# Deformable convolution main loop: distances and caps for two steps at a time, batches of eight, tap matmuls in two runs a block

## What is computed

```python
py = off_y + hs[None, None, :, None] + ky[None, :, None, None]
px = off_x + ws[None, None, None, :] + kx[None, :, None, None]
y0, x0 = jnp.floor(py), jnp.floor(px)
...
sampled = v00 * w00 + v01 * w01 + v10 * w10 + v11 * w11   # bilinear, zero outside the image
sampled = sampled * mask[:, None]
out = jnp.einsum('bckhw,ock->bohw', sampled, w.reshape(O, C, KK))
```

## Time and profile before

| what | value |
|---|---|
| median of three runs | 2331.67 us |
| lowest, highest run | 2330.77, 2337.22 us |
| span of the profiled execution, first to last instruction | 2334.2 us |
| PE, weight loads, DVE, ACT, POOL busy over the span | 66%, 45%, 67%, 62%, 26% |
| mean granted TensorE clock over the span | 0.846 |
| main loop, from the first `keep_even` to the last block | 701.8 to 2105.2 us |
| in it: PE, DVE, ACT, POOL busy | 1230.8, 1198.9, 1228.6, 570.8 us of 1403.4 |

### The profile page before, as it was taken

How to read it: one execution, slowest core, us unless ns; L and a number is a source line. 1 busy time by engine, 2 the same in 40 slices (tenths; PEclk the granted TensorE clock), 3 DMA queues, 4 the chain that set the end, 5 groups by cost and what they waited for, 6 DMA issues and landing times. The chain is left out here.

```text
span 2334.2 us, 61913 instructions
## 1 busy us (share of the span) xinstructions
PE 1539.5 (66%) x24206; PEld 1050.0 (45%) x24207; DVE 1558.4 (67%) x1718; ACT 1449.8 (62%) x2219; POOL 606.7 (26%) x1168
## 2 busy tenths in 40 slices
PE   4755980000008888888898898898888898891620
PEld 4632330000006666666665566666665666660310
DVE  5342006656717888888888788888887888883105
ACT  2221224344218898888898898898887898890102
POOL 2000000000033444444443444444444444430000
PEclk9688995555558999999999999999999999996555
DMA  2177874667675666666666666566666656640008
GB/s 116 32 190 184 233 218 159 215 227 275 235 214 126 151 147 157 149 149 155 150 148 152 148 149 157 149 150 157 149 146 150 152 147 157 149 100 22 3 0 338
DMA packets 288861, 362.19 MB, mean 155 GB/s; under 512 B 61853, under 2 KB 260820, under 8 KB 285014
## 3 DMA queue, kind: packets, MB, share of 16 engines
q1 hardware_dynamic: 209552, 226.57, 37.6%
q0 software_dynamic: 36864, 59.94, 11.2%
q10 hardware_dynamic: 42182, 72.05, 9.0%
HBM read 253.94 MB, written 104.39 MB: 154 GB/s over the span
## 5 line engine op out<-in xcount | busy, mean ns | idle before, releaser
L758 POOL DMA_DIRECT2D rows<-scratch_parts x1152 | 583.1, 514 | 821.1 <-PE ps_even_y L790 798.8
L799 PE MATMUL ps_odd_y<-rows,sel 32*128 32x504 f32 (+2 forms) x928 | 459.8, 496 | 502.5 <-DMA rows<-scratch_parts 345.2
L939 DVE TENSOR_TENSOR G<-odd_y,ps_odd_v 128x1008 f32<-128x1008 f32 (+2 forms) x464 | 542.0, 1168 | 182.5 <-PE ps_odd_v L816 182.4
L816 PE MATMUL ps_odd_v<-tent_x,stage 32*128 32x171 f32 (+2 forms) x5568 | 591.1, 318 | 0.0
L947 DVE TENSOR_TENSOR G<-even_v,ps_even_y 128x1008 f32<-128x1008 f32 (+2 forms) x464 | 539.3, 1162 | 23.6 <-ACT even_v L895 21.7
L816 PE MATMUL ps_even_v<-tent_x,stage 32*128 32x171 f32 (+3 forms) x5568 | 541.9, 324 | 8.5 <-DMA stage<-scratch_xt 8.3
L889 ACT COPY odd_y<-ps_odd_y 128x504 f32<-128x504 f32 (+2 forms) x928 | 526.4, 567 | 21.4 <-PE ps_odd_y L799 17.1
L895 ACT COPY even_v<-ps_even_v 128x1008 f32<-128x1008 f32 (+2 forms) x464 | 450.2, 970 | 134.6 <-PE ps_odd_v L816 126.5
L834 PE MATMUL ps_r<-G,conv_w 128*32 128x224 f32 (+1 forms) x8832 | 483.3, 346 | 13.2 <-ACT res L900 13.1
L799 PEld LDWEIGHTS ps_odd_y<-rows,sel 32*128 32x128 f32 x928 | 173.0, 186 | 689.8 <-issue 350.5
L816 PEld LDWEIGHTS ps_odd_v<-tent_x,stage 32*128 32x128 f32 x5568 | 477.8, 190 | 0.0
(11 more groups left out here) (134 smaller groups left out, 913.5 us busy)
## 6 DMA issues: line engine op xcount, KB each, us to landing
place<-scratch_px SPq DMA_DIRECT2D x960, 105.0 KB, 3.4
scratch_parts<-parts ACTq DMA_DIRECT2D x18, 3136.0 KB, 16.7
rows<-scratch_parts POOLq DMA_DIRECT2D x960, 52.5 KB, 3.4
x<-scratch_xh SPq DMA_DIRECT2D x48, 406.0 KB, 5.9
place<-scratch_px SPq DMA_DIRECT2D x192, 84.0 KB, 2.7
scratch_om<-om ACTq DMA_DIRECT2D x64, 196.0 KB, 7.1
rows<-scratch_parts POOLq DMA_DIRECT2D x192, 42.0 KB, 2.6
scratch_conv<-res SPq DMA_DIRECT2D x448, 14.0 KB, 1.8
```

What stands on the lines that cost most here:

```text
L758: pool.dma_start(bass.AP(tensor=rows[b][:].tensor, offset=32 * g * pitch + here, ap=[[2 * pitch, Y_KINDS], [GROUP * W, 3], [1, count * W]] ...
L799: nc.tensor.matmul(ps_odd_y[:, lo:hi], sel[32 * g:32 * g + 32, :], taps(rows, 32 * g, 32, p, lo, hi), start=True, stop=True).then_inc(odd_ ...
L816: m = nc.tensor.matmul(sub(ps_v[g // 2], 0, 128, i * 512 + lo + first, dims), stage[32 * g:32 * g + 32, j * IMAGE + v * C:j * IMAGE + (v + ...
L939: nc.vector.tensor_tensor(two(G, ROW, v, slot(v)), two(odd_y[p % 3], ROW, v), two(ps_v[1], 512, v), ALU.mult).then_inc(odd_weighted, 1)
```

## The change

Three things change in the main loop, and one beside it.

1. `distance` and `cap` handle two steps in one instruction. `dist_x` and `tent_x` hold 9 taps by two steps (1008 columns) in two buffers rather than 504 columns in three. A pair has 15 such twins, the last with a single step. They are issued in odd steps: step p computes the twin of steps p+3 and p+4; steps 27 and 28 compute the first two twins of the next pair.
2. Batches have 8 steps, not 5: four a pair (8, 8, 8, 5), with the same two buffers, so `place` and `rows` are loaded with 48 DMAs each a pair in place of 72, of 1.6 times the size.
3. A block's taps run in two runs, not four: in the second of its four steps taps 0 to 3, in the fourth taps 4 to 8. The first and third steps have none.
4. `zeros` shrinks, to make room; the far stage stores its pads in more, smaller DMAs.

```diff
-GROUP = 5
+GROUP = 8
...
-        zeros = sb("zeros", XT_ROWS * C)
+        zeros = sb("zeros", NEAR * C)
...
-            dist_x = [sb(f"dist_x{b}", ROW) for b in range(3)]
-            tent_x = [sb(f"tent_x{b}", ROW) for b in range(3)]
+            dist_x = [sb(f"dist_x{b}", 2 * ROW) for b in range(2)]
+            tent_x = [sb(f"tent_x{b}", 2 * ROW) for b in range(2)]
...
+            def twin(it, p):
+                return (STEPS + 1) // 2 * it + p // 2
+            def twin_steps(p):
+                return min(2, STEPS - p)
+            def sampled_by(n):
+                return STEPS * (n // TWINS) + min(2 * (n % TWINS + 1), STEPS)
+            def next_twin(it, p, last):
+                if p % 2 == 1 and p + 3 < STEPS:
+                    return it, p + 3
+                if p in (STEPS - 2, STEPS - 1) and not last:
+                    return it + 1, 2 * (p - STEPS + 2)
+                return None
...
-                                sp.wait_ge(distant, STEPS * it + p + 2)
+                                sp.wait_ge(distant, twin(it, p + 1) + 1)
...
-                    pe.wait_ge(tent_ready, n + 1)
+                    pe.wait_ge(tent_ready, twin(it, p) + 1)
...
-                        if at := block_of(it, p):
-                            if at[2] == 0:
+                        if (at := block_of(it, p)) and at[2] % 2:
+                            if at[2] == 1:
                                 pe.wait_ge(even_weighted, STEPS * at[0] + BLOCK // 2 * (at[1] + 1) + 1)
+                            reduce(at[0], at[1], at[2] - 1)
                             reduce(*at)
                         if to:
                             spread_odd(*to, 1)
...
                 def distance(it, p):
-                    n = STEPS * it + p
+                    n = twin(it, p)
...
                     wait(act, tent_ready, n - 1)
-                    lo, hi = both(p)
-                    nc.scalar.activation(sub(dist_x[p % 3], 0, 128, lo, [[W, (hi - lo) // W], [1, W]]),
-                                         taps(place, 0, 128, p, lo, hi), ACT.Abs, bias=at[:, 0:1]).then_inc(distant, 1)
+                    dims = [[2 * W, KK], [1, twin_steps(p) * W]]
+                    nc.scalar.activation(sub(dist_x[n % 2], 0, 128, 0, dims),
+                                         sub(place[p // GROUP % 2], 0, 128, p % GROUP * W, [[GROUP * W, KK], dims[1]]),
+                                         ACT.Abs, bias=at[:, 0:1]).then_inc(distant, 1)
...
-                        if to := ahead(it, p + 2, last):
+                        if (to := next_twin(it, p, last)):
                             distance(*to)
...
                 def cap(it, p):
-                    n = STEPS * it + p
+                    n = twin(it, p)
                     dve.wait_ge(distant, n + 1)
-                    wait(dve, sampled, n - 1)
...
+                    if n >= 2:
+                        dve.wait_ge(sampled, sampled_by(n - 2))
...
-                        if to := ahead(it, p + 2, last):
+                        if (to := next_twin(it, p, last)):
                             cap(*to)
```

More of the change, by code:

```diff
@@ L644, in program @@
             ASKED = {first + count - 2: n for n, (first, count) in enumerate(BATCHES)}
+            TWINS = (STEPS + 1) // 2
             block = st.enter_context(nc.Block())
@@ L651, in columns, with twin_part @@
                 return first * 3 * W, end * 3 * W
-            def both(p):
-                return columns(2 * p)[0], columns(2 * p + 1)[1]
+            def twin(it, p):
[4 more added lines that the diff above has]
+                return STEPS * (n // TWINS) + min(2 * (n % TWINS + 1), STEPS)
+            def twin_part(tile, part, parts, p, lo, hi, first, count):
+                return sub(tile, part, parts, lo * 2 + p % 2 * W + first, [[2 * W, (hi - lo) // W], [1, count]])
             def two(tile, pitch, v, offset=0):
@@ L814, in sample @@
                             lo, hi = columns(v)
-                            dims = [[W, (hi - lo) // W], [1, count]]
-                            m = nc.tensor.matmul(sub(ps_v[g // 2], 0, 128, i * 512 + lo + first, dims),
+                            m = nc.tensor.matmul(sub(ps_v[g // 2], 0, 128, i * 512 + lo + first, [[W, (hi - lo) // W], [1, count]]),
                                                  stage[32 * g:32 * g + 32, j * IMAGE + v * C:j * IMAGE + (v + WIN) * C],
-                                                 sub(tent_x[p % 3], 32 * g, 32, lo + first, dims), start=True, stop=True)
+                                                 twin_part(tent_x[twin(it, p) % 2], 32 * g, 32, p, lo, hi, first, count),
+                                                 start=True, stop=True)
                     m.then_inc(sampled, 1)
@@ L903, in _ @@
                 keep_odd(0, 0, 0)
-                distance(0, 1)
+                distance(0, 2)
                 keep_odd(0, 0, 1)
@@ L950, in cap @@
                 def cap(it, p):
-                    n = STEPS * it + p
+                    n = twin(it, p)
                     dve.wait_ge(distant, n + 1)
-                    wait(dve, sampled, n - 1)
-                    lo, hi = both(p)
-                    nc.vector.tensor_scalar(tent_x[p % 3][:, lo:hi], dist_x[p % 3][:, lo:hi], 1.0, 1.0,
-                                            ALU.min, ALU.subtract).then_inc(tent_ready, 1)
+                    if n >= 2:
+                        dve.wait_ge(sampled, sampled_by(n - 2))
+                    if twin_steps(p) == 2:
+                        here = [tile[n % 2][:, :] for tile in (tent_x, dist_x)]
+                    else:
+                        here = [sub(tile[n % 2], 0, 128, 0, [[2 * W, KK], [1, W]]) for tile in (tent_x, dist_x)]
+                    nc.vector.tensor_scalar(here[0], here[1], 1.0, 1.0, ALU.min, ALU.subtract).then_inc(tent_ready, 1)
                 cap(0, 0)
-                cap(0, 1)
+                cap(0, 2)
                 def body(it, last):
@@ L1057, in _ @@
                     for a, z in ((0, TOP - NEAR), (TOP + H + NEAR, XT_ROWS)):
-                        sp.dma_start(dram("xt", a * C, [[XT_ROW, W], [W * XT_ROW, B], [1, (z - a) * C]]),
-                                     sub(zeros, 0, W, 0, [[0, B], [1, (z - a) * C]])).then_inc(S["x_pads"], 16)
-                    sp.wait_ge(S["x_pads"], 32)
+                        for first in range(a, z, NEAR):
+                            sp.dma_start(dram("xt", first * C, [[XT_ROW, W], [W * XT_ROW, B], [1, NEAR * C]]),
+                                         sub(zeros, 0, W, 0, [[0, B], [1, NEAR * C]])).then_inc(S["x_pads"], 16)
+                    sp.wait_ge(S["x_pads"], 16 * 2 * (TOP - NEAR) // NEAR)
                 sp.nop()
```

## The result

The changed kernel takes 2531.74 us (2530.06 to 2534.57) beside 2334.44 us for the kernel before in the same measurement, a ratio of 1.0838 [1.0815, 1.0861]: 8.4% slower, and 42 us past the upper end of the range that was predicted. The profiled execution took 2530.72 us, its span is 2528.9.

The account below looks back on a forecast made before the run. The prediction took a ring of waits between PE and ACT, 2.94 us a step, as the bound. Its terms 111 + 5 + 10 − 35 = +91 raised the span from 2334.2 to 2425, median 2423 us, range 2385 to 2490.

Parts of the forecast that it names:

- Tap matmuls in two runs, +111 us: Main loop: runs of four and five taps delay the odd spread by 0.31 and 0.69 us, 1.00 us a block.
- the rule on drains: Tap runs: changing the tiling mode drains the engine, so two runs fewer a block would make the sum 45 us lower.
- the long runs don't fit the gap: Rival, 5%: merged tap runs fit PE's gap, taps cost 0.24 us or less, and the kernel gets faster, 2312 us.
- no stall could pay for them: Rival, 3%: the odd spread starts 0.6 us before a long run's end, stalls pay for the delays, 2330 us, no change.
- Distances and caps, +5 us, from 0 to 10: Odd steps on ACT: the longer distance lets the next `keep_even` start at 2.965 us, 13 odd steps in 16 pairs.
- the ring: Main loop: PE and ACT wait for each other, from `keep_even` to odd spread to next `keep_even`, 2.94 us once round.
- PE waiting for `odd_y` only in tapless steps: Sign in the new trace: PE waits for ACT's copy of `odd_y` in steps without taps and in no others.
- Batches of eight, −35 us: Loads on SP and POOL: fewer issues let the store come in time and remove stalls, from −15 to −45 us.
- the 47 us of stalls: Steps 3 to 5 and 12 and 13 over 16 pairs: time beyond 2.94 us a step, 34.4 + 12.6 us.
- one fall in half the pairs, 8 us: Tapless steps 4 and 5: the clock's fall to 1.2 GHz, seen in pair 1, stays in half the pairs.
- a fall in every second tapless step, 125 us: Rival, 12%: the clock falls in tapless steps, 240 in all, 120 falls of 1.04 us, giving 2548 us.
- Start, +10 us: Before the loop: larger fills of `rows` add 2.6 us, the 24 loads of `place` 6.8 by bytes; from 2.6 in all.

Follow-up runs that it names:

- e5: The kernel before with the tap matmuls in two runs and nothing else changed; 2468.01 us, ratio 1.0573 to the kernel before.
- e2: The changed kernel with distances and caps of one step each again, batches of eight and two tap runs kept; 2529.02 us, ratio 1.0849 to the kernel before.
- e3: The kernel before with batches of eight and smaller `zeros` only; 2412.72 us, ratio 1.0361 to the kernel before.
- e4: The changed kernel with eight matmuls of no use in every tapless step, so PE isn't idle there; 2486.54 us, ratio 1.0674 to the kernel before.
- e1: The changed kernel with a block's taps in four runs again, twins and batches of eight kept; 2409.34 us, ratio 1.0333 to the kernel before.
- e6: e3 with the store moved ahead of the loads in SP's list of a step; 2378.26 us, ratio 1.0177 to the kernel before.
- e7: The kernel before with the store moved ahead of the loads in SP's list of a step; 2295.24 us, ratio 0.9828 to the kernel before.
- e9: e6 with the 12 loads of a batch spread over four steps (two where needed soon), both `place` and `rows`; 2403.70 us.
- e11: e6 with only the loads of `place` spread over several steps, `rows` still in one burst; 2401.04 us.
- e8: e7 with eight matmuls of no use in step 4, the one step without taps; 2288.90 us, ratio 0.9800 to the kernel before.

## Why the prediction was wrong

**Tap matmuls in two runs, +111 us: right.** Runs of 1.72 and 2.12 us, steps of 3.24 and 3.64 us in e5 (forecast 3.25 and 3.63), tapless steps still 2.94. Over 14 tap steps a pair that is 110 us. By the rule on drains that I set against this term it would have been 45 lower; the runs don't show that gain. Two rivals are out with it: the long runs don't fit the gap, and the next odd spread starts only 0.06 and 0.07 us before their end (1556.54, 1563.44), so no stall could pay for them.

**Distances and caps, +5 us, from 0 to 10: the first step that failed.** The length of a distance was right (1.149 us for 1.155), that of a cap too (0.69 us, hidden). The step went wrong where I wrote that the next `keep_even` "could start at 1.37 + 1.155 − 0.04 + 0.58 − 0.10 = 2.965, 0.025 past the ring". I asked what the late second `keep_odd` does to ACT's next instruction, and not who else waits for it. PE's first odd spread of the next step does, and the taps stand behind that spread in PE's list. Before a tapless step this is hidden, before a run that already ends late it isn't: 0.34 us in a four-tap step and, step for step, 0.33 in a five-tap step (falls in step 20 of e2 make it 0.30 in the table), 3.3 us a pair by the step lengths, about 53 us in the loop. Of my signs, "PE waiting for `odd_y` only in tapless steps" is the one that this breaks.

**Batches of eight, −35 us: the second, wrong in its sign.** I followed the store through SP's list and found it "comes in time". By SP's list it does, in e3 too, but there it then waits behind the bytes of a larger burst, and the same burst delays PE's instructions. Alone the batches cost 83 us (e3), the start in it; on top of the two runs they lengthen the loop by 45 us (e2 beside e5). And the 47 us of stalls weren't theirs to bring: in the changed kernel `result` waits for no store, as I had written, but it doesn't in e5 either, with batches of five, because its longer steps leave the store more time. I added two terms that pay for the same stalls. In place of the 47 us that are gone 64 have come (180.5 for the loop is 163 of step lengths, below, less 47, plus 64). e4 gives back 41 of them; what the other 23 are I haven't separated.

**The clock: the third, mis-sized.** I left one fall in half the pairs, 8 us, and gave 12% to a fall in every second tapless step, 125 us. It came between them: 42 falls, 41 to 45 us. The falls belong to the tapless steps and not to the batches, for e5 has 48. Part of the long steps 1 and 3 is of this kind: step 3 takes 5.3 us in four pairs, each time with a fall in it, where 3.6 is usual; step 1 takes 4.0 to 7.1 us in six pairs, and in three of these the clock is low for a part of it.

**Start, +10 us: right in size,** 11.5, but not in its parts. The fills cost 2.5 us for 2.6 and the issue of `place` 4.9 for 6.8; the landing of the first `stage` band came 6.4 us later on top of that, and that the stage ahead of the loop ended 2.4 us earlier was luck.

**The sum.** The loop grew by 180.5 us in place of 81. By step lengths 163 of it are the tap steps (110 for the two runs, 53 for the twins), where the forecast had 116; the stalls and the clock make +18, where it had −35. That is 47 and 53 us, which with 1.5 of the start is the distance from the forecast span of 2425 to the 2528.9 of the profile, but for 2 us. The forecast had the direction, for the largest term was right; two others failed in their mechanism.

What this sum doesn't settle: alone, two runs cost 132 us and batches 83, and twins on top of both cost nothing in time (e2 and the changed kernel agree within their intervals), although they lengthen the steps by 53 us in all. So the 53 us are shown for the lengths of single steps, and not as time that the kernel gains without the twins; e1 and e3 show the same (2409.34 and 2412.72), although the twins lengthen five steps a pair of e1 by 0.24. In e2 the shorter steps go with 17 more falls, 72 us more at the lower clock. Why the clock falls in steps 11 to 21 of e2 and e5 and not of the changed kernel stays open. Spread loads and the store moved ahead weren't tried on the changed kernel as a whole. Nor is it separated whether the size of the loads does the harm or their place: with batches of eight every load of `place` (steps 6, 14, 22, 27) comes a step ahead of a load of `stage` (7, 15, 23, 28), with batches of five three of six lie that close, and spreading them changes both.

## What to carry to other kernels

An instruction that grows delays whatever stands behind it on its engine: follow that late instruction to every engine that waits for it, one step further than its own engine's next start. A small transfer in time by its queue's list can still land late: ask how many bytes stand in the DMA engines at that moment, from all queues, and move the small store ahead or spread the loads rather than enlarge them. PE idle time that costs nothing in its own step may bring the clock down in it and in the steps after it (42 falls in the changed kernel, 4 with the gaps filled), so price a gap by the granted clock too. And two terms of a sum can both claim the same stall: ask of each what is left of it once the others have happened.

## What the runs showed that I had not expected

Fewer, larger loads of the same bytes were dearer than more, smaller ones: e6 and e7 differ in the batches alone (and the smaller `zeros` that make room for them), and by 83 us, some 13 of them the longer start. A burst of loads can hold up the program itself: PE stood still for up to 3.3 us, with an instruction packet in flight as each of the eight longest stops of its matmuls in e6 began, and the stops at taps and sampling went away when the loads of `place` were spread (e9 and e11, 0.5 us at most). And matmuls of no use made a kernel faster: eight in one step a pair by 6 us (e8 beside e7, 2295.24 to 2288.90), eight in each tapless step by 45 us (e4 beside the changed kernel).
